# Values and gates by a seven-product scheme, with the last output adds on VectorE and the first loads moved up

## What is computed

```python
xn = _layernorm(x)
q = xn @ Wq                                   # 512 -> 128
gate = softmax(xn @ Wg)                       # 512 -> 3
for i in range(3):
    k, v = xn @ Wk[i], xn @ Wv[i]             # 512 -> 128 each
    scores = (q @ k.T) * decay_i**(distance)  # strictly causal
    blended += gate[..., i:i+1] * (scores @ v)
s = blended @ Wo * out_scale
h = silu(xn @ w_gate.T) * (xn @ w_up.T)       # 512 -> 1376, weights are lut[idx]
out = x + s * silu(h @ w_down.T)
```

## Time and profile before

| | |
|---|---|
| median of 3 runs | 1812.95 us (1812.1 to 1813.01) |
| profiled execution | 1813.45 us, span of its instructions 1811.5 us |
| TensorE busy | 1773.3 us, 98% |
| VectorE, GpSimd, ScalarE busy | 76%, 57%, 46% |
| TensorE's share of the chain that ended last | 93% |
| values and gates (line 1825) | 768 matmuls, 7.9 us a group |

### The profile page before, as it was taken

The page is one execution under the profiler, slowest core; times in us unless marked ns, Lnnn a source line. Parts: engine busy times, 40 slices in busy tenths (PEclk is TensorE's granted clock), DMA queues, the critical chain, the costliest instruction groups (busy, mean ns, idle before and its releaser), DMA issues.

```text
span 1811.5 us, 43135 instructions
## 1 busy us (share of the span) xinstructions
PE 1773.3 (98%) x16520; PEld 1476.6 (82%) x16520; DVE 1379.0 (76%) x2719; ACT 827.1 (46%) x1442; POOL 1038.4 (57%) x1041
## 2 busy tenths in 40 slices
PE   5999999999999999999999999999999999999997
PEld 2337888888888988888888888888898888888886
DVE  7897877777786878777787777778687777868684
ACT  3785444444444444454444444444444444444433
POOL 9303746656474755647474664647476564747263
PEclk9999999999999999999999999999999999999999
DMA  9986686968868686877968696886959687786753
GB/s 224 331 306 167 178 226 164 258 170 211 217 173 232 175 241 168 239 192 186 229 172 231 169 262 165 208 218 173 237 163 253 166 225 199 184 238 166 214 153 108
DMA packets 411033, 370.99 MB, mean 205 GB/s; under 512 B 222576, under 2 KB 278640, under 8 KB 410752
## 3 DMA queue, kind: packets, MB, share of 16 engines
q1 hardware_dynamic: 399824, 361.36, 73.2%
q0 software_dynamic: 11008, 6.89, 2.5%
HBM read 294.34 MB, written 35.52 MB: 182 GB/s over the span
## 4 chain that ended last, share of the span: by engine, by line
PE 93%; ACT 2%; DMA 2%; POOL 1%; DVE 1%; issue 1%; POOLq 0%; SPq 0%; DVEq 0%; ACTq 0%
PE F L1931 52%; PE F L1994 20%; PE B L1825 7%; PE F L1975 2%; PE B L1857 2%; PE B L1830 2%; PE B L1832 2%; PE B L1831 2%; PE F L1732 1%; POOL codes L756 1%; PE F L1830 1%; PE F L1831 1%; PE F L1832 1%; ACT ring L950 1%; DMA dblocks<-xt 1%
## 5 line engine op out<-in xcount | busy, mean ns | idle before, releaser
L1931 PE MATMUL F<-xtc,ring 128*128 128x256 f16 (+1 forms) x4224 | 497.7, 273 | 0.0
L1931 PEld LDWEIGHTS F<-xtc,ring 128*128 128x128 f16 (+1 forms) x4224 | 415.9, 100 | 42.5
L1994 PE MATMUL F<-ring,region 128*128 128x256 f16 x3360 | 382.5, 273 | 0.0
L1931 PE MATMUL F<-xt,ring 128*128 128x256 f16 (+1 forms) x3168 | 377.2, 273 | 0.0
L1994 PEld LDWEIGHTS F<-ring,region 128*128 128x128 f16 x3360 | 327.9, 98 | 47.9
L1931 PEld LDWEIGHTS F<-xt,ring 128*128 128x128 f16 (+1 forms) x3168 | 310.9, 100 | 33.2
L950 ACT ACTIVATE region<-region 128x512 f16<-128x512 f32 (+3 forms) x304 | 160.3, 527 | 283.2 <-DVE region L1606 115.8
L860 POOL TENSOR_TENSOR region<-hs,region 128x1024 f16<-128x1024 f32 x80 | 175.2, 2190 | 104.2 <-ACT region L950 104.2
L950 ACT ACTIVATE region<-F 128x512 f32<-128x512 f32 (+1 forms) x200 | 114.7, 575 | 101.1 <-PE F L1931 50.6
L868 POOL TENSOR_TENSOR faded<-state,fade_tile 128x384 f32<-128x384 f32 x56 | 46.3, 827 | 180.7 <-DVE region L1504 180.7
L878 POOL TENSOR_TENSOR x_out<-x_out,region 128x512 f32<-128x512 f32 x64 | 84.4, 1318 | 96.9 <-DVE region L1677 96.9
(11 more groups left out here) (265 smaller groups left out, 3438.6 us busy)
## 6 DMA issues: line engine op xcount, KB each, us to landing
ring<-blocks SPq DMA_DIRECT2D x546, 256.0 KB, 3.3
ring<-dblocks SPq DMA_DIRECT2D x224, 256.0 KB, 3.4
x_next<-in_x SPq DMA_DIRECT2D x64, 256.0 KB, 3.7
x_out<-in_x SPq DMA_DIRECT2D x64, 256.0 KB, 3.2
out_y<-x_out SPq DMA_DIRECT2D x64, 256.0 KB, 5.5
ring<-blocks SPq DMA_DIRECT2D x112, 128.0 KB, 2.5
ring<-dblocks SPq DMA_DIRECT2D x112, 128.0 KB, 3.1
blocks<-ring SPq DMA_DIRECT2D x35, 256.0 KB, 7.0
```

The source lines that it names most:

```text
L1931: ins = T_.matmul(out_, a, b, start=fresh, stop=False, skip_group_check=True)
L1994: ins = T_.matmul(bank[:, j * HV:(j + 1) * HV], a, b, start=fresh, stop=False, skip_group_check=True)
```

## The change

Values and gates become a set `VG` of the same seven-product scheme. The four banks `B` take its seven products; x and the sums of x in `xtc` stay stationary, the weights and their sums move. Its right-hand matrix has 387 columns, made 388 by a column of zeros, so a half is `VH` = 194 wide; a product is 2 tiles of 128 tokens by 2 blocks by 3 terms, 12 matmuls of 194 columns. The first copy and the five combinations are those of the other sets. The output comes in four quarters of 2 tiles by 194 (or 193) columns (`VGB`); the scaled version is now made straight out of each quarter, in two pieces by head (`PIECE`), on both engines, and `vb32` goes. Its sums of weights are made in the set-up and at the start of group 0. `x_sums_high(0)` moves behind the exponential. The next group's x tiles use two slots of `xhat_half` instead of four. In the last group VectorE does the adds of x for output blocks 2 and 3. SyncE's three small loads and GpSimd's first three loads move ahead of the counter steps.

```diff
+    VH = (NH * D + NH + 1) // 2
+    VBASE = {A11: (0, CV), A12: (2, CV), A22: (2, CV + VH), S4: (0, CV + VH)}
...
+        XB[VG], YB[VG], ZB[VG] = (v[:, :, 0:VH] for v in (XC[1], SC[0], SC[1]))
...
+        VGB = ((ZB[VG], 1, 2), (vbank[0].rearrange("p (m t) -> p m t", m=2)[:, :, 0:VH], 0, 0), (YB[VG], 0, 2),
+               (XB[VG], 1, 0))
+
+        PIECE = (((0, 0, D), (1, D, VH)), ((1, 0, 2 * D - VH), (2, 2 * D - VH, HD - VH)))
+        WIDE = (VH, HD - VH)
...
         def _(sp):
+            sp.dma_start(lutrow[:, :], lut.partition_broadcast(P)).then_inc(s_small, 16)
+            sp.dma_start(dlog[:, :], decay_logits.partition_broadcast(P)).then_inc(s_par, 16)
+            sp.dma_start(oscale[:, :], out_scale.partition_broadcast(P)).then_inc(s_par, 16)
             for t in range(GT):
                 sp.sem_inc(s_y[t], 16 * FREE)
...
+            for b in range(UNR):
+                load_direct(b)
             pool.sem_inc(s_hl1, 2 * FREE)
...
-                finish(2)
-                finish(3)
+                if not last:
+                    finish(2)
+                    finish(3)
...
                 first_copy(QK)
+                if gi == 0:
+                    act.wait_ge(s_dwr[ND - 1], 16)
+                    for n in range(4, 8):
+                        act.wait_ge(s_scale, 2 + n + 1)
+                        copy(qs_half(n, 0), sums[n]).then_inc(s_ahi, 1)
...
-                for t in range(GT):
-                    act.wait_ge(s_pv, gi * GT + t + 1)
-                    copy(v_hi[:, t], B[VB[t]][:, 0:HD], scale=2.0 ** QP).then_inc(s_v, 1)
-                    copy(logit[:, t], B[VB[t]][:, HD:HD + NH], scale=f_down[:, 3:4]).then_inc(s_lg, 1)
-                    act.wait_ge(s_vb, gi * GT + t + 1)
-                    copy(vb_hi[:, t], vb32[:, :]).then_inc(s_vbh, 1)
-                    if t in XSUMHI and not last:
-                        x_sums_high(XSUMHI[t])
+                def v_high(n):
...
+                    act.wait_ge(*done)
+                    copy(v_hi[:, t0:t0 + 2, c0:c0 + w], block[:, :, 0:w], scale=2.0 ** QP).then_inc(s_v, 1)
+                    if half:
+                        copy(logit[:, t0:t0 + 2], block[:, :, w:w + NH], scale=f_down[:, 3:4]).then_inc(s_lg, 1)
+
+                def vb_high(n):
+
+                    block, half, t0 = VGB[n]
+                    for hd, a, b in PIECE[half]:
+                        c = half * VH + a
+                        copy(vb_hi[:, t0:t0 + 2, c:c + b - a], block[:, :, a:b], scale=fade_v[:, hd:hd + 1]).then_inc(s_vbh, 1)
+
+                first_copy(VG)
...
+                for n in range(4):
+                    v_high(n)
+                    vb_high(n)
...
+                    if n == 1 and not last:
+                        x_sums_high(0)
...
+            for m in (a32, a_hi, a_lo):
+                step(V_.memset(m[:, :, QKV:QKV + 1], 0.0))
...
+            weight_sums(((0, slice(0, CK)), (1, slice(CK, CV))), 0, 2 * P, 2 * P, 0)
+            sums_low(0, 2)
+            weight_sums(((2, slice(CV, CGT)), (3, slice(CGT, QKV))), CV, CV + VH, VH, 4)
+            sums_low(2, 4)
...
                 c22(QK)
+                if gi == 0:
+                    sums_low(4, 8)
...
-                for t in range(GT):
-                    dve.wait_ge(s_lg, gi * GT + t + 1)
-                    if t:
-                        dve.wait_ge(s_vbl, gi * GT + t)
-                    V_.tensor_tensor(heads(vb32[:, :]), heads(B[VB[t]][:, 0:HD]), spread(fade_v),
-                                     ALU.mult).then_inc(s_vb, 1)
-                    V_.scalar_tensor_tensor(out=v_lo[:, t], in0=B[VB[t]][:, 0:HD], scalar=2.0 ** QP, in1=v_hi[:, t],
-                                            op0=ALU.mult, op1=ALU.subtract).then_inc(s_vl, 1)
-                    dve.wait_ge(s_vbh, gi * GT + t + 1)
-                    V_.tensor_tensor(vb_lo[:, t], vb32[:, :], vb_hi[:, t], ALU.subtract).then_inc(s_vbl, 1)
+                def v_low(n):
...
+                    V_.scalar_tensor_tensor(out=v_lo[:, t0:t0 + 2, c0:c0 + w], in0=block[:, :, 0:w], scalar=2.0 ** QP,
+                                            in1=v_hi[:, t0:t0 + 2, c0:c0 + w], op0=ALU.mult,
+                                            op1=ALU.subtract).then_inc(s_vl, 1)
+                    dve.wait_ge(s_vbh, (gi * 4 + n + 1) * 2)
+                    for hd, a, b in PIECE[half]:
+                        c = half * VH + a
+                        V_.scalar_tensor_tensor(out=vb_lo[:, t0:t0 + 2, c:c + b - a], in0=block[:, :, a:b],
+                                                scalar=fade_v[:, hd:hd + 1], in1=vb_hi[:, t0:t0 + 2, c:c + b - a],
+                                                op0=ALU.mult, op1=ALU.subtract).then_inc(s_vbl, 1)
+
+                u2(VG)
+                u4(VG)
+                c22(VG)
+                v_low(0)
+                c12(VG)
+                v_low(1)
+                c21(VG)
+                v_low(2)
+                v_low(3)
...
-                product_out(2)
-                product_out(3)
+                for n in (2, 3):
+                    product_out(n)
+                    if last:
+                        finish(n)
...
-                    for done in (s_lg, s_vl, s_vbl, s_qkl):
-                        pe.wait_ge(done, gi * GT + GT)
+                    pe.wait_ge(s_qkl, gi * 4 + 4)
+                    pe.wait_ge(s_u2, of_set(gi, VG) + 1)
...
+                        if s == VG:
+
+                            toks = slice(n * P, (n + 1) * P)
+                            sh, sl, mh, ml = mh[:, toks], ml[:, toks], sh, sl
...
-                    three(B[VB[t]], [(xh[:, k, cols], xl[:, k, cols], a_hi[:, k, CV:QKV], a_lo[:, k, CV:QKV])
-                                         for k in range(KC)], HD + NH).then_inc(s_pv, 1)
+                for p in range(NP):
+                    product(i, g, VG, p)
```

More of the change, by code:

```diff
@@ L314, in attention_ffn_kernel @@
         build = UNR * CG * CG * BANK * 2
-        region = sb("region", [P, max(sum(sizes.values()), build + KC * QKV * 4 + 16 * BANK * 2) // 4], F32)
+        region = sb("region", [P, max(sum(sizes.values()), build + KC * (QKV + 1) * 4 + 16 * BANK * 2) // 4], F32)
         at = {}
@@ L320, in attention_ffn_kernel @@
             pos += n
+        B = [ps("B0"), ps("B1"), ps("B2"), ps("B3")]
+        vbank = [v[:, :] for v in B]
         fb = ctx.enter_context(nc.psum_tensor("F", [P, 4, BANK], F32))
@@ L739, in _, with load_direct @@
             G_ = nc.gpsimd
+            def load_direct(b):
+                rows = idx[UNITS[b][1]].rearrange("p q c -> p (q c)").unsqueeze(1).broadcast_to([QR, CG, CG * BANK])
+                pool.dma_start(codes[b].rearrange("p q c -> p (q c)"), rows).then_inc(s_first[b], 16)
+            for b in range(UNR):
+                load_direct(b)
             pool.sem_inc(s_hl1, 2 * FREE)
@@ L744, in _ @@
             pool.sem_inc(s_hsl, FREE)
-            def load_direct(b):
-                rows = idx[UNITS[b][1]].rearrange("p q c -> p (q c)").unsqueeze(1).broadcast_to([QR, CG, CG * BANK])
-                pool.dma_start(codes[b].rearrange("p q c -> p (q c)"), rows).then_inc(s_first[b], 16)
-            for b in range(UNR):
-                load_direct(b)
             def cast(u, c, col, w, done):
@@ L1677, in product_out, with finish @@
                     V_.tensor_tensor(block, block, attn[:, t0:t0 + 2, v0:v0 + HV], ALU.mult).then_inc(s_y1, 1)
+                def finish(n):
+                    block, v0 = ((C22, HV), (C21, 0))[n - 2]
+                    to = x_out[:, 0:2, v0:v0 + HV]
+                    dve.wait_ge(s_y1, gi * GT + n + 1 + GT)
+                    dve.wait_ge(s_yr, gi * GT + n + FREE)
+                    V_.tensor_tensor(to, to, block, ALU.add).then_inc(s_yr, 1)
                 def next_xhat(j):
@@ L1854, in retrieve @@
                     pe.wait_ge(s_mix, (gi * GT + n + 1) * NMIX)
+                else:
+                    pe.wait_ge(s_vl, gi * 4 + 4)
+                    pe.wait_ge(s_vbl, (gi * 4 + 4) * 2)
                 if n or g:
@@ L1906, in product @@
                     pe.wait_ge(s_c22, prev + 1)
-                if s != QK:
+                if s == QK and p in (3, 5):
+                    pe.wait_ge(s_alo, len(MATS) + (3 if p == 3 else 4))
+                if s == VG:
+                    bank = vbank[FB.index(bank)]
+                if s >= 0:
                     slot = ring_slot(g, s * NP + p)
@@ L1911, in weights @@
                 def weights(n, k):
-                    if s != QK:
+                    if s >= 0:
                         w, M = MW[s], FM[MS[s][n]]
                         return [ring[:, slot // NP, slot % NP, hl, k * w + n * P:k * w + n * P + M] for hl in range(2)]
+                    if s == VG:
+                        if p in QSUM:
+                            return [qs_half(4 + QSUM[p], lo)[:, k] for lo in range(2)]
+                        kb, c0 = VBASE[p]
```

(3 more changed lines are left out.)

136 lines of the change are left out of this document (79 added, 57 removed).

## The result

The kernel after takes 1793.73 us (median of 4 runs, 1792.32 to 1795.78) beside 1812.98 us of the kernel before (4 runs): a ratio of 0.9899, 95% interval [0.9885, 0.9912]. That is 19.2 us, where 14.6 were forecast, and 1.8 us under the range's lower end of 1795.5. The mechanism of the stage came out as argued. What was missed is the end of the kernel.

The account below looks back on a forecast made before the run. TensorE, busy for 98% of the span, was taken as the bound. Steady groups 13.8, group 0 0, start 0.2 and end 0.6 sum to 14.6 us, so 1812.95 becomes 1798.4 us, range 1795.5 to 1804.5 (about 8 in 10).

Parts of the forecast that it names:

- The bound and the price of the stage: Values and gates: TensorE is the bound; 84 matmuls at 83.2 ns take 6.99 us for 7.91, 0.92 us less a group.
- No new wait in the steady groups: Groups 1 to 15: other engines still deliver in time, so 15 x 0.92 = 13.8 us is gained; chance 0.72.
- the add for the sixth product of set 0: VectorE's add, done 13.05 us after the stage's start, needed by TensorE at 14.0: slack 1.0 us.
- The low part of the probabilities: VectorE's step before retrieval 0: waits for GpSimd's low part, runs 15.6 to 16.1 us, needed at 16.7: slack 0.6 us.
- Group 0: First group: VectorE's added work uses up the stage's saving; gain 0, between 0.9 us gained and 2 us lost.
- VectorE's backlog: Group 0: added low parts and set-up operations on VectorE make TensorE wait up to 1.9 us more in the stage.
- the later steps would have slack again: Group 0: the wait at the scores goes, and set 0's fourth product comes at 163.6 us, where it is now.
- The start: Set-up: loads ahead of counter steps start up to 1.4 us earlier; 0.2 us gained, between 0 and 1.4.
- the load that the step named as cover: Set-up: later table codes behind GpSimd's queue of casts, for which VectorE idles 3.12 us; takes nearly all the start's gain.
- The end: Last group: final add takes 0.69 us on VectorE for 1.26 on GpSimd, so the run is 0.6 us shorter.
- the only risk: End of kernel: if the start's cover were gone and the output's transfer ended on something else, the 0.6 us would be 0.
- The sum: Whole kernel: 13.8 + 0 + 0.2 + 0.6 = 14.6 us less, profiled execution 1798.85 us, median 1798.4 us.

Follow-up runs that it names:

- experiment 11: Kernel after with VectorE's four one-column scalings of the output scale moved behind the softmax of group 0: 1794.06 us, ratio 0.9897 to the kernel before.
- experiment 7: Kernel after with VectorE's low sums in group 0 split around two combinations and TensorE waiting piece by piece: 1795.15 us, ratio 0.9904 to the kernel before.
- The timed pairs: Early loads alone in the kernel before (0.0 us), undone in the kernel after (0.3), and with against without them, last adds undone in both (0.8).
- experiment 8: The kernel after, unchanged, run again beside the kernel before: 1794.82 us, ratio 0.9898.
- experiment 6: Kernel after with one more GpSimd instruction at its end, a one-column memset nothing reads, waiting for VectorE's last add: 1799.6 us.

## Why the prediction was wrong, point by point

**The bound and the price of the stage: right.** 84 matmuls of 194 columns were priced at 83.2 ns by the line through 128 and 256 columns, and take 83.5. A group gains 0.90 us for 0.92, and fifteen of them 12.58 + 0.90 = 13.5 for 13.8. By the page "TensorE: Matmul & The Clock Gate" of the Trainium skill, section "Back-to-back issue gap", the stage would have taken 7.5 us (an estimate from that page's figures for a stream of pairs of weight load and matmul); the trace has 7.01 and disagrees.

**No new wait in the steady groups: right, with less to spare than argued.** The add for the sixth product of set 0 ends at 983.88 + 0.69 - 971.59 = 13.0 us into the stage (forecast 13.05). The low part of the probabilities ends at 16.4 for 16.1. The step let it wait for the end of GpSimd's part, and it did, but by way of the gate operation just ahead, which met that part and took 1.25 us. The need at 16.7 was right, so 0.26 us of slack is left of 0.6.

**Group 0: gain 0 forecast, 1.07 us lost**, inside the bounds given (0.9 gained to 2 lost). By the other traces the loss lies between 0.6 and 2.1 us. TensorE waits 2.8 us there for 1.08 before. The step's cause, VectorE's backlog, is what experiment 11 confirmed and experiment 7 showed by moving the wait instead of removing it. That the later steps would have slack again, so that the group gains its 0.9 us back, was the part that did not come.

**The start: 0.2 us forecast (0 to 1.4).** The first comparison of codes on VectorE comes 3.4 us earlier in after, and the comparison behind the load that the step named as cover 4.0 us. Timeline of VectorE up to 36 us, where the view ends in the midst of that row's four instructions, against the earlier trace rows:

```profile
35.03 1.47 DVE L1325 TENSOR_SCALAR region<-xt,code 128x2048 f16<-128x2048 f16 x2 [1.35 <-DMA xt<-codes]
```

Over all traces of experiments that row starts at 34.7 to 36.4 with the loads ahead and at 37.3 to 39.0 with them behind, so the cover did not hold as I put it: it moved too, by some 2.5 us. By the means of the table above 1.3 to 1.6 us of it is left at the first queries, and 1.8 to 2.1 between traces with the same idle stretch and the same clock. The timed pairs give 0.0, 0.3 (0.7 by the ratios, since the two ran beside different runs of the kernel before) and 0.8 us. That the start is worth something between 0 and 1.5 us is all that they tell; why they give less than the marks stays open.

**The end: 0.6 us forecast, 4.4 us measured. This is the step that failed.** It took the difference of the two adds (1.26 and 0.69) as the whole price, and named as the only risk that the transfer would end last. Neither add nor transfer ended last before: GpSimd's DRAIN did, 8.08 us long. For the path that the step looked at, 0.6 us was right: SyncE's stores are through 5.7 us behind the last matmul before and 5.1 after. The other 3.8 us are the DRAIN that went on beyond them. With 4.4 in place of 0.6 the forecast would have been 18.4 us for the measured 19.2, inside the interval. The trace of before had it: the last pieces of the chain in order of time (start us, us, what) end in GpSimd's queue, and the span ended 7 us behind SyncE's last store issue.

```profile
1800.09 1.26 POOL x_out L878
1801.35 1.81 issue
1803.16 1.30 POOLq L210
```
I read the chain's shares and the row of the add, and not what each engine's queue did after it. The page "Runtime: NRT & Kernel Launch" of the Trainium skill, section "The ~15µs preamble/postamble breakdown", gives about 1.5 us for the closing barrier, in which all engines are waited for. The traces here have 6.8 us from GpSimd's last instruction to the end of its queue alone; whether the two are the same stage no run here shows.

**The sum.** With the measured terms it is 13.5 - 1.07 + 4.4 and 0 to 1.5, 16.8 to 18.3 us, so 1794.7 to 1796.2. The 19.2 us of the first comparison lie 0.9 to 2.4 above that, with an interval of 16 to 21 us; the second comparison, experiment 8, gives 18.1. The profiled execution of before, on which the sum was made, has the fall of the clock in its set-up and that of after hasn't; I had not asked whether that execution was a typical one. Of the 21.0 us between the two traces the 4.2 us of set-up are therefore in part luck of which execution was profiled.

## What to carry to other kernels

Read the end of a program from the closing instructions of every engine, not from the last work: here an engine whose DRAIN is long should get its last instruction early, and a small last operation is worth moving to another engine for that alone. Price a matmul in a stream by start to start at neighbouring widths; here that came within 0.4%. Where runs of one kernel scatter by more than the effect looked for, look for the stretch in which their traces differ before asking for more runs: here it was, by all signs, one idle stretch of TensorE, which could be filled.

## What was not expected of the hardware

- GpSimd's closing DRAIN ends 6.8 us after its last instruction (8.08 us from the start of an add of 1.26 us in the trace before, 6.88 from the start of a memset of 0.10 us in experiment 6). Those of ScalarE, VectorE and TensorE last 0.72, 0.73 and 2.16 us in the trace before and end within 0.1 us of the end of the last work of their engine.
- The granted clock fell to the 1.2 GHz level behind idle stretches of TensorE of 2.4 to 3.0 us in 8 of 12 traces and not in the other 4, and between traces that are otherwise alike the set-up was 1.8 to 3.6 us longer with the fall. In the two traces in which the stretch was 0.6 or 0.7 us it did not fall there.
- VectorE's subtractions with two SBUF inputs of 128x388 took 0.56 us, and 1.08 to 1.51 beside a GpSimd operation in the trace of after; one in experiment 11 took 0.56 beside one, too. An operation of 12 columns took 1.25 us in most groups of after, with GpSimd's low part of the x sums beside it, for 0.17 in the trace before, without.
